# A four-block transformer kernel whose norms, projections, turned residuals and sums are signalled piece by piece

## The reference

```python
# block 0: cross attention to the 64 context tokens, 16 heads of 16
q  = ada_ln(x, cond) @ Wq + bq;  kv = ada_ln(ctx, cond) @ Wkv + bkv
x  = x + softmax(q k^T / 4) v @ Wp + bp
# block 1: evidence from the context, router over 3 experts (768 -> 512 -> 256), gate
nx = ln(x) * gamma + beta
evidence = softmax(nx Wq (ctx Wk)^T / 16) (ctx Wv)
combined = [nx, evidence, cond]
routed = sum_e router_e(combined) * expert_e(combined)
x  = x + gate(combined) * (routed @ out_w + out_b)
# block 2: full self attention over 1024 tokens, cross attention, MLP of 1024
x  = x + gate_a * (self_attention(ada(ln(x))) @ W_proj + b_proj)
x  = x + cross_attention(ln(x), ln(ctx)) @ W_cproj + b_cproj
x  = x + gate_m * (gelu(ada(ln(x)) @ W1 + b1) @ W2 + b2)
# block 3: attention in windows of 128 tokens shifted by 64,
#          cross attention to the 16 best of 64 context tokens, SwiGLU MLP of 1024
x  = x + g_msa * window_attention(ada(ln(x)))
x  = x + g_mca * topk_cross_attention(ada(ln(x)), ctx)
x  = x + g_mlp * swiglu(ada(ln(x)))
```

## Time and profile before

| what | value |
|---|---|
| device time, median of 3 runs | 1791.75 us (1786.18 to 1791.81) |
| profiled execution, its own time | 1789.12 us |
| its span, first to last instruction | 1787.0 us |
| mean granted TensorE clock | 0.951 of full speed |
| TensorE busy | 1575.8 us, 88% of the span |
| VectorE busy | 1082.2 us, 61% |
| ScalarE busy | 812.6 us, 45% |
| GpSimd busy | 417.7 us, 23% |
| transfers | 64.02 MB, mean 36 GB/s |

### The profile page before, as it was taken

How to read it: one execution, slowest core, us unless ns; L and a number is a source line. 1 busy time by engine, 2 the same in 40 slices (tenths; PEclk the granted TensorE clock), 3 DMA queues, 4 the chain that set the end, 5 groups by cost and what they waited for, 6 DMA issues and landing times.

```text
span 1787.0 us, 27133 instructions
## 1 busy us (share of the span) xinstructions
PE 1575.8 (88%) x9541; PEld 917.6 (51%) x9541; DVE 1082.2 (61%) x2933; ACT 812.6 (45%) x1283; POOL 417.7 (23%) x418
## 2 busy tenths in 40 slices
PE   3789998999988989877878899899998888987888
PEld 1536564434343756455653556543443365654566
DVE  1464243899726338799536433479991643879963
ACT  1134331388843535324533434138886353442454
POOL 0140003433006024113205000153300602412230
PEclk8799999999999999999998999999999999999899
DMA  9200004422010000000050000352201000000004
GB/s 318 95 1 1 0 1 135 61 38 38 2 71 1 1 1 2 1 1 1 1 166 2 1 1 1 111 84 38 38 2 72 1 1 1 2 1 1 1 1 141
DMA packets 43332, 64.02 MB, mean 36 GB/s; under 512 B 8634, under 2 KB 32061, under 8 KB 42301
## 3 DMA queue, kind: packets, MB, share of 16 engines
q1 hardware_dynamic: 32845, 40.73, 6.9%
q0 software_dynamic: 8448, 14.96, 5.6%
q10 hardware_dynamic: 1904, 6.55, 0.9%
HBM read 47.28 MB, written 2.10 MB: 28 GB/s over the span
## 4 chain that ended last, share of the span: by engine, by line
PE 38%; issue 37%; POOL 12%; DVE 8%; ACT 3%; SPq 2%; DMA 1%; POOLq 0%; ACTq 0%; DVEq 0%
PE ps L932 7%; PE ps L944 7%; PE ps L1188 4%; PE ps L448 3%; POOL wkblk L2396 3%; PE ps L1022 3%; PE ps L917 3%; PE ps L1030 2%; PE ps L565 2%; PE ps L1217 2%; DVE taken L2198 2%; DVE taken L2210 1%; POOL rstd L2292 1%; DVE m L2193 1%; PE ps L457 1%
## 5 line engine op out<-in xcount | busy, mean ns | idle before, releaser
L2067 DVE TENSOR_REDUCE mm<-ps 128x1 f32<-128x1024 f32 x256 | 309.6, 1223 | 36.7 <-PE ps L917 30.0
L1490 ACT ACTIVATE pt<-ps 128x512 f32<-128x512 f32 x512 | 276.9, 598 | 62.8 <-PE ps L932 53.6
L2292 POOL TENSOR_TENSOR rstd<-ve,minus_half 128x4 f32<-128x4 f32 x32 | 36.2, 1130 | 810.7 <-DVE ve L1800 810.7
L932 PE MATMUL ps<-qx,kx 64*128 64x512 f32 x512 | 192.0, 452 | 1.8 <-ACT pt L1490 1.0
L917 PE MATMUL ps<-kx,qx 48*128 48x512 f32 x512 | 189.5, 450 | 1.7 <-DVE mm L2067 1.7
L944 PE MATMUL ps<-pt,v 128*32 128x256 f32 x2048 | 161.2, 396 | 0.0
L932 PEld LDWEIGHTS ps<-qx,kx 64*128 64x128 f32 x512 | 80.0, 186 | 98.2 <-ACT pt L1490 92.9
L1956 DVE TENSOR_TENSOR rlo<-ring,rhi 128x512 fp32r<-128x512 f32 x48 | 33.2, 692 | 127.7 <-ACT ring L1441 127.6
L917 PEld LDWEIGHTS ps<-kx,qx 48*128 48x128 f32 x512 | 76.6, 187 | 25.8 <-issue 15.4
L944 PEld LDWEIGHTS ps<-pt,v 128*32 128x32 f32 x2048 | 43.3, 109 | 87.8 <-ACT pt L1490 63.7
L457 PE MATMUL ps<-ident,xhat 128*128 128x128 f32 x288 | 45.0, 309 | 44.9 <-DVE xhat L1805 43.2
(11 more groups left out here) (322 smaller groups left out, 3454.0 us busy)
## 6 DMA issues: line engine op xcount, KB each, us to landing
w<-in_L_xcond_e_w_dram SPq DMA_DIRECT2D x9, 512.0 KB, 8.0
w<-in_L_xcond_e_w_dram SPq DMA_DIRECT2D x3, 1536.0 KB, 12.1
wm<-in_L_xcond_W_mlp_dram SPq DMA_DIRECT2D x4, 1024.0 KB, 7.9
qx<-q_hi POOLq DMA_DIRECT2D x64, 64.0 KB, 2.6
kx<-k_hi POOLq DMA_DIRECT2D x64, 64.0 KB, 2.8
w3a<-in_L_xcond_w_m_dram SPq DMA_DIRECT2D x2, 2048.0 KB, 8.1
s_ada<-in_L_xcond_w_ada_dram ACTq DMA_DIRECT2D x1, 2304.0 KB, 14.7
qx<-q_lo POOLq DMA_DIRECT2D x32, 64.0 KB, 2.6
```

The source lines that it names most:

```text
L932: pe.matmul(ps[:, bank, :], kx[r, p % 4, kc * P:(kc + 1) * P], qx[r, p % 4, half * 512:(half + 1) * 512], start=True, stop=True).then_inc( ...
L1490: act.activation(pt[:, u % 8, half * 512:(half + 1) * 512], ps[:, bank, :], ACT.Exp, scale=QK_SCALE).then_inc(st_read, 1)
L2067: return dve.tensor_reduce(mm[:, p % 2, e, t:t + 1], place(), X, ALU.max).then_inc(ring_read, 1)
L2292: pool.tensor_tensor(rstd[:, k, :], ve[:, k, :], minus_half[:, :], ALU.pow).then_inc(rstd_ready, 1)
```

## The change

Semaphores that were raised once for a block, or once for two banks, are raised once for each piece, and the waits on them count pieces.

- `xhat_ready`: once for each tile. TensorE's `ln` waits for each tile and transposes both of its halves; `ln_turned` stays one for the block. `turn_block` is gone; the attention's outputs are turned half by half, with `ot_turned` raised for each.
- `hT_ready`: once for each feature half. `linear` takes a pair `each`, and waits for half c in front of its matmul on half c, in the first bank of a projection. Consumers that are not written so wait for both halves.
- Norms 4 and 7 on ScalarE: both high parts first, each with a semaphore raise (`hs2_hi`, new; `hs3_hi`), then both halves of `hT`. TensorE waits for `hs2_hi` or `hs3_hi` half by half; `tokens3_lo` waits for `hT_ready` in place of `hs3_hi`.
- `q_done` and `y_done`: once for each bank; ScalarE evicts a bank as soon as it is done. `qk3_done`: once for each of four banks.
- `yT_ready`: once for each feature half. TensorE's turn has the feature half outside and the tiles inside, and waits for each half; for residuals (0, 1), (1, 0) and (4, 0) it waits for both first (`whole`). `y_turned`: once for each PSUM bank, and VectorE adds in two instructions on 128x512, a bank each.
- Banks move: the norm behind a context attention goes to bank 2i (i: first or second), the turn of residual (5, 0) to bank 2, of (6, 0) to bank 4, of (6, 1) to bank 0, of (7, 0) to bank 2, of (7, 1) to bank 4.

The core of the diff (the waits that only count in new units are left out):

```diff
-    def linear(bank, w, m, src):
+    def linear(bank, w, m, src, each=None):
         for c in range(KC):
+            if each is not None:
+                pe.wait_ge(each[0], each[1] + c + 1)
             ins = pe.matmul(ps[:, bank, :], w[:, c, m * P:(m + 1) * P], src[:, c, :],
                             start=c == 0, stop=c == KC - 1)
         return ins
...
-            pe.wait_ge(xhat_ready, b * 2 * N_LN + 2 * i + k + 1)
-            turn_block(k, xhat, bank).then_inc(ln_turned, 1)
+            bank = 4 * k if bank is None else bank
+            for t in range(TB):
+                pe.wait_ge(xhat_ready, b * 2 * N_LN * TB + (2 * i + k) * TB + t + 1)
+                for c in range(KC):
+                    ins = pe.transpose(ps[:, bank + c, t * P:(t + 1) * P], xhat[:, TB * k + t, c * P:(c + 1) * P], ident[:, :])
+            ins.then_inc(ln_turned, 1)
         def query(i, k, ln_i, w):
-            pe.wait_ge(hT_ready, b * (2 * N_LN + 2) + ln_i + k + 1)
-            linear(4 * k + 2, w, 0, hT[:, k])
+            linear(4 * k + 2, w, 0, hT[:, k], (hT_ready, b * 2 * N_HT + 2 * (ln_i + k))).then_inc(q_done, 1)
             linear(4 * k + 3, w, 1, hT[:, k]).then_inc(q_done, 1)
-        def residual(i, k, turn, w=None, o_wait=None, src=oT, bank=None):
+        def residual(i, k, turn, w=None, o_wait=None, src=oT, bank=None, each=None, whole=False):
             if not turn:
                 bank = 4 * k + 2 if bank is None else bank
-                pe.wait_ge(*o_wait)
-                linear(bank, w, 0, src[:, k])
+                if o_wait is not None:
+                    pe.wait_ge(*o_wait)
+                linear(bank, w, 0, src[:, k], each).then_inc(y_done, 1)
                 linear(bank + 1, w, 1, src[:, k]).then_inc(y_done, 1)
             else:
                 bank = 4 * k if bank is None else bank
-                pe.wait_ge(yT_ready, b * 2 * N_RES + 2 * i + k + 1)
-                for t in range(TB):
-                    for c in range(KC):
+                for c in range(KC):
+                    if not whole or c == 0:
+                        pe.wait_ge(yT_ready, b * 4 * N_RES + 2 * (2 * i + k) + (KC if whole else c + 1))
+                    for t in range(TB):
                         ins = pe.transpose(ps[:, bank + t // 2, t % 2 * D + c * P:t % 2 * D + (c + 1) * P],
                                            yT[:, k, c, t * P:(t + 1) * P], ident[:, :])
-                ins.then_inc(y_turned, 1)
+                        if c == KC - 1 and t % 2:
+                            ins.then_inc(y_turned, 1)
...
-            residual(step, 1, False, w, (co_ready, u0 + 4), bank=4)
-            ln(step + 1, 0)
+            residual(step, 1, False, w, bank=4, each=(co_ready, u0 + KC))
+            ln(step + 1, 0, bank=2 * i)
...
-            turn_block(k, xhat).then_inc(ot_turned, 1)
+            for c in range(KC):
+                for t in range(TB):
+                    ins = pe.transpose(ps[:, 4 * k + c, t * P:(t + 1) * P], xhat[:, TB * k + t, c * P:(c + 1) * P], ident[:, :])
+                ins.then_inc(ot_turned, 1)
-        residual(2, 0, False, wproj, (hT_ready, b * (2 * N_LN + 2) + 7), hT)
-        pe.wait_ge(hT_ready, b * (2 * N_LN + 2) + 8)
-        linear(6, wproj, 0, hT[:, 1])
+        residual(2, 0, False, wproj, src=hT, each=(hT_ready, b * 2 * N_HT + 12))
+        linear(6, wproj, 0, hT[:, 1], (hT_ready, b * 2 * N_HT + 14)).then_inc(y_done, 1)
         linear(7, wproj, 1, hT[:, 1]).then_inc(y_done, 1)
...
+                    if m == 0 and (wp, sp) == (0, 0):
+                        pe.wait_ge(hs2_hi, b * NB * KC + k * KC + c + 1)
...
-                ins = linear(4 * k + m, wqkv3, m, hT[:, k])
+                linear(4 * k + m, wqkv3, m, hT[:, k], (hT_ready, b * 2 * N_HT + 2 * (12 + k)) if m == 0 else None).then_inc(qk3_done, 1)
 -                    ins.then_inc(qk3_done, 1)
...
+                            if each and (i, wp) == (0, 0):
+                                pe.wait_ge(hs3_hi, b * NB * KC + k * KC + c + 1)
...
+            def evict(dst, c):
+                if cols is None:
+                    return act.activation(dst, ps[:, bank + c, :], ACT.Copy)
+                table, scale, bias = cols
+                return affine(dst, ps[:, bank + c, :], table[:, scale + c:scale + c + 1], table[:, bias + c:bias + c + 1])
+            def high(c):
+                return hs1[:, k, c, :] if i == 1 else hs[:, k, 0, c, :] if i == 4 else hs3[k][:, c, :]
+            if i in (4, 7):
+                for c in range(KC):
+                    evict(high(c), c).then_inc(hs2_hi if i == 4 else hs3_hi, 1)
             for c in range(KC):
-                if cols is None:
-                    ins = act.activation(hT[:, k, c, :], ps[:, bank + c, :], ACT.Copy)
-                else:
-                    table, scale, bias = cols
-                    ins = affine(hT[:, k, c, :], ps[:, bank + c, :], table[:, scale + c:scale + c + 1], table[:, bias + c:bias + c + 1])
-                if i == 4:
-                    ins = affine(hs[:, k, 0, c, :], ps[:, bank + c, :], table[:, scale + c:scale + c + 1], table[:, bias + c:bias + c + 1])
-            ins.then_inc(hT_ready, 1)
+                evict(hT[:, k, c, :], c).then_inc(hT_ready, 1)
             if i == 1:
                 for c in range(KC):
-                    ins = affine(hs1[:, k, c, :], ps[:, bank + c, :], table[:, scale + c:scale + c + 1], table[:, bias + c:bias + c + 1])
+                    ins = evict(high(c), c)
                 ins.then_inc(hs1_hi, 1)
-            if i == 7:
-                for c in range(KC):
-                    ins = affine(hs3[k][:, c, :], ps[:, bank + c, :], table[:, scale + c:scale + c + 1], table[:, bias + c:bias + c + 1])
-                ins.then_inc(hs3_hi, 1)
         def query(i, k, col):
-            act.wait_ge(q_done, b * 2 * N_Q + 2 * i + k + 1)
             for c in range(KC):
+                act.wait_ge(q_done, b * 4 * N_Q + 2 * (2 * i + k) + c + 1)
                 ins = affine(qT[:, k, c, :], ps[:, 4 * k + 2 + c, :], 1.0, colT[:, col + c:col + c + 1])
             ins.then_inc(qT_ready, 1)
-        def residual(k, bank, scale, bias):
+        def residual(k, bank, scale, bias, done=None):
             for c in range(KC):
-                ins = affine(yT[:, k, c, :], ps[:, bank + c, :], 1.0 if scale is None else mod[:, scale + c:scale + c + 1],
-                             bias[:, c:c + 1])
-            ins.then_inc(yT_ready, 1)
+                if done is not None:
+                    act.wait_ge(y_done, b * 24 + 2 * done + c + 1)
+                affine(yT[:, k, c, :], ps[:, bank + c, :], 1.0 if scale is None else mod[:, scale + c:scale + c + 1],
+                       bias[:, c:c + 1]).then_inc(yT_ready, 1)
...
             for t in range(TB):
-                ins = dve.tensor_scalar(xhat[:, TB * k + t, :], x[:, TB * k + t, :], mv[:, k, t, 0:1], rstd[:, k, t:t + 1], ALU.subtract, ALU.mult)
-            ins.then_inc(xhat_ready, 1)
+                dve.tensor_scalar(xhat[:, TB * k + t, :], x[:, TB * k + t, :], mv[:, k, t, 0:1], rstd[:, k, t:t + 1], ALU.subtract, ALU.mult).then_inc(xhat_ready, 1)
         def residual(i, k, bank=None):
             bank = 4 * k if bank is None else bank
-            dve.wait_ge(y_turned, b * 2 * N_RES + 2 * i + k + 1)
-            return dve.tensor_tensor(x[:, TB * k:TB * (k + 1), :].rearrange("p t d -> p (t d)"),
-                                     x[:, TB * k:TB * (k + 1), :].rearrange("p t d -> p (t d)"),
-                                     ps[:, bank:bank + 2, :].rearrange("p a n -> p (a n)"), ALU.add)
+            for j in range(TB // 2):
+                dve.wait_ge(y_turned, b * 4 * N_RES + 2 * (2 * i + k) + j + 1)
+                two = x[:, TB * k + 2 * j:TB * k + 2 * j + 2, :].rearrange("p t d -> p (t d)")
+                ins = dve.tensor_tensor(two, two, ps[:, bank + j, :], ALU.add)
+            return ins
...
-            dve.wait_ge(y_done, b * 12 + 2 + k + 1)
             for m in range(KC):
-                ins = dve.scalar_tensor_tensor(yT[:, k, m, :], ps[:, 2 + 4 * k + m, :], colT[:, C_OUTB + m:C_OUTB + m + 1], gT[:, k, m, :], ALU.add, ALU.mult)
-            ins.then_inc(yT_ready, 1)
+                dve.wait_ge(y_done, b * 24 + 2 * (2 + k) + m + 1)
+                dve.scalar_tensor_tensor(yT[:, k, m, :], ps[:, 2 + 4 * k + m, :], colT[:, C_OUTB + m:C_OUTB + m + 1], gT[:, k, m, :], ALU.add, ALU.mult).then_inc(yT_ready, 1)
...
```

96 lines of the change are left out of this document (40 added, 56 removed).

## The result

The changed kernel takes 1738.88 us (median of 4, 1735.72 to 1745.49), the kernel before beside it 1789.12 (1786.18 to 1791.81). The ratio is 0.9722, 95% interval 0.969 to 0.9754: 50 us less. In the profiled executions 1789.12 became 1735.72.

What follows compares the result with a forecast made beforehand. TensorE, busy 88% of the span, bounds the long loops; the rest is hand-overs between stages. Terms sum to 17.3 us per batch, 34.6 in two, less 1.6 for unmet waits: 33, giving 1757 us (range 1741 to 1780).

Steps and rivals of the forecast that it cites:

- start of the batch, first residual: Earlier transposes, projection and query evictions at batch start, 2.5 us per batch; first context attention's residual add earlier, about 0.85.
- experts to attention: Between experts and attention: per-bank add gives 0.3 and the norm's turn 0.7, together 1.0 us per batch.
- norm 3 and query: Attention to second context attention: normalisation 1.35 us earlier, turn 1.0, one eviction less 0.55, query 0.5 and 0.3; 3.7 per batch.
- norm 4, both MLP blocks: Norm behind the second context attention: 0.7 us from transposes, 0.4 from high parts first, the low parts coming as before.
- window, queries and keys: Window attention, both blocks: per-bank eviction cuts TensorE's 2.5 us idle before the value projection to 0.69; 3.5 per batch.
- window to top-k: Between window and top-k: turns 0.8 us, query eviction 0.6, one norm eviction 0.6, less 0.1; 1.9 per batch.
- last MLP block 1, last add: Batch end: high parts first gain 0.6 us in the last MLP's block 1; overlapped half-turn and add gain 0.7.
- the chains named as late next: At each hand-over, the neighbouring work that would end last after the change and cap the gain, such as VectorE's own product.
- the rows that were to show them: Signs: value-projection gap about 0.7 us, norm 3's transposes within 0.1 of first tile, normalisation within 0.2 of add's end, loops unchanged.
- Norm 7's first block gains nothing: Norm 7, block 0: no gain, because fillers hold TensorE before it and GpSimd's subtraction holds it behind.
- The clock rises too: Rival: shorter gaps keep TensorE at 2.4 GHz in second value projection and query behind attention; 7.4 us more, 1749; chance 0.13.
- Slower, by the clock in the long loop: Rival: the attention loop, reached earlier, falls to 1.2 GHz; with 80 us low the time is 1797; chance 0.06.

Runs made afterwards that it cites:

- whole: The changed kernel with every piecewise wait put back to the last piece, keeping increments, split adds and moved banks: 1787.82 us, 0.9997 of the kernel before.
- the filled pair: The changed kernel, and `whole`, each with constant-tile matmuls where TensorE idles (in `whole` also in both window gaps): 1728.42 and 1768.89 us.
- gap_filled: `whole` with nine constant-tile matmuls ahead of the window stage's second value projection: 1782.22 us, 0.9967 of the kernel before.
- high: `whole` with only the high parts first in norms 4 and 7, waited for half by half: 1794.55 us, 1.0028 of the kernel before.
- whole_n7: `whole` with 13 constant-tile matmuls ahead of the turn in front of norm 7: 1797.74 us, 1.0037 of the kernel before.
- window: `whole` with only the window stage's queries and keys evicted bank by bank: 1781.45 us, 0.9981 of the kernel before.
- no_window_filled: The changed kernel with window queries and keys evicted whole again, and nine constant-tile matmuls in each window gap: 1750.16 us, 0.9777 of the kernel before.
- the first try: The changed kernel with window queries and keys evicted whole again, and 13 constant-tile matmuls ahead of norm 7: 1752.01 us, 0.9798 of the kernel before.
- warm3: The changed kernel with constant-tile matmuls at three gaps per batch, small groups at five more, and 13 ahead of norm 7: 1724.11 us, 0.9641.

## Why the prediction was too small

By the starts of GpSimd's powers, which every norm block has, and by the first and last matmul of the attention loop and the first scores of the second context attention between them, the change can be read place by place in the two profiled executions (us gained, batch 1 / batch 2):

| place | forecast | measured |
|---|---|---|
| set-up, once | 0 | 2.5 |
| start of the batch, first residual | 3.3 | 3.4 / 3.6 |
| norm 1 | 0.7 | 0.7 / 0.7 |
| experts to attention | 1.0 | 3.1 / 3.2 |
| attention loop | 0 | -0.1 / 0.8 |
| attention's outputs turned | 0 | 1.9 / -0.9 |
| norm 3 and query | 3.7 | 3.0 / 2.6 |
| second residual | 0.8 | 1.2 / 1.2 |
| norm 4, both MLP blocks | 1.1 | 2.8 / 2.4 |
| window, queries and keys | 3.5 | 4.3 / 4.3 |
| window to top-k | 1.9 | 2.8 / 4.7 |
| norm 7, block 0, and first products | 0 | 3.1 / 0.1 |
| last MLP block 1, last add | 1.3 | 0.9 / 1.2 |

The measured rows come to 27.1 and 23.9, with the set-up to 53.5 (the spans differ by 53.2; the rest is rounding); the forecast's to 17.3 twice. The medians differ by 50, since the changed kernel's profiled execution is its fastest. The set-up's 2.5 are not the change's: no edit touches it, and it took 74.9 to 77.7 over the profiled kernels, 76.0 in `whole`.

**Right: what bounds it, and the chains named as late next.** Start of batch, residuals, norm 3, window gaps and the last add came within about a us of their terms, and the rows that were to show them did: the gap in front of the values 0.78, the transposes of norm 3 0.47 behind the first tile's start (a tile takes 0.4), normalisation 0.12 behind its add's end (and 1.3 behind the end of the block's statistics, before 2.4: 1.1 gained where 1.35 was forecast), an add pair 1.28, a loop of 202.6. One term inside norm 3 was mis-sized: the turn was to end 0.4 behind the last tile and gain 1.0. It ended 1.06 behind it, before 1.40, for its eight transposes now took 1.97 and not 1.34, the low clock; 0.3 was gained.

**Right: increments are free.** `whole` has all of them and runs at 0.9997. The Trainium skill's 26.3 ns an increment (TensorE: Matmul & The Clock Gate, "The cost: per-tile semaphore tail") would have shown as 2.2 us there, 0.0012 of the time; the interval reaches 1.0006. So no such price shows in the time here.

**Failed: "Norm 7's first block gains nothing: fillers hold TensorE before it, GpSimd's subtraction behind it".** Both chains were there, but the fillers' own length wasn't looked at. They ran at the low clock in batch 1 of the kernel before, had shown such a stretch elsewhere, and batch 2 of the same trace had the fast case. A comparison of the two batches would have shown 61.1 against 58.1. Measured were 3.1 in batch 1 and 0.1 in batch 2.

**Failed: the clock as a rival instead of a term.** "The clock rises too" was priced at 7.4 at two places and given 0.13, as if it excluded the forecast. It adds to the hand-overs: the second value projection (1.7 in each batch) did come as that rival had it, the query projection behind norm 3 hardly (5.67 for 6.18). By the filled pair, 8 of the 49 against `whole` are clock at the least. The two traces allow an estimate from the places seen, both batches together: norm 7's first block 3.2, second value projections 3.4, experts stage 3.0, the projection behind norm 2's second block 2.6 (6.54 and 6.45 became 5.29 and 5.09), the MLP's first twelve matmuls 2.5 (5.17 and 4.63 became 3.66 and 3.65), the query behind norm 3 0.5. That is 15, beside the 14.7 us by which TensorE's busy time fell. So the size of the miss, 18 us, is the clock for the most part. Which of these levels the change brought about, and which another execution of the same kernel would not have, isn't shown; that of the experts stage stood in `whole` as well.

**Slightly too small at most: the hand-overs.** 33 were forecast. The filled pair gives 40.5 as an upper bound; less the 4 of the experts stage it is 36.5, and the 53.2 of the traces less the set-up's 2.5 and the 15 of clock are 36 as well (an estimate). Two rows of the table that look like it are clock beyond their forecast: experts to attention, 3.1 for 1.0, with 1.5 from the experts stage and 1.25 from the projection; and the MLP, 2.8 for 1.1, with 1.5 from its first matmuls. There, high parts first did let TensorE start 2 us earlier and VectorE's subtraction 0.65 earlier. The 4.7 for 1.9 from the window to top-k in batch 2 is not placed.

**The slower rival exists.** "Slower, by the clock in the long loop" was given 0.06. It didn't happen here, but three profiled executions (`gap_filled`, `high`, `whole_n7`) have a loop of 217 instead of 202 at a clock of 0.91. It costs 14 to 15 us at a time, there in batch 1 only; the other 31 loops profiled have 0.97 or 0.98. Of the executions that were timed, those over 12 us above their kernel's lowest are 9 of the 36 of `window`, `gap_filled` and `high`, 8 of the 12 of `whole_n7`, 1 of the 23 of the kernel before in the second set, and none of the 4 of the changed kernel. That all of them are this loop is not shown: `no_window_filled`'s profiled execution lies 12.4 above its lowest with a loop of the usual length.

**Open.** What makes that loop fall to 0.91, with the same code before it in `whole` (0.98); what decides whether the fillers ahead of norm 7 run fast, beyond how long TensorE stood before them; what sets the clock of the experts stage; and how often each level comes, since only one execution of each kernel is profiled.

## What to carry to other kernels

Signal a hand-over in pieces wherever both engines handle it in pieces anyway: the extra increments cost nothing measurable here, and each place gives its link's length less one piece, up to the chain that is late next. Price the clock of every TensorE-bound stretch as a term of the sum: compare the same stage in two iterations of a loop, since a difference between them (61.1 and 58.1 here) is what that stage may win or lose without an edit of its own. Don't judge such a part alone: the same edits brought 6 alone and 22 in company, or -6 and 11.

## What the runs showed of the hardware

- VectorE's `tensor_scalar` on 128x256 f32, four of them, took 1.38 alone and 4.55 beside GpSimd's `tensor_tensor` on 128x1024 (3.80 for two), which itself lost nothing (3.75 before). In `window` alone it was 4.53. The Trainium skill (GPSIMD Engine Reference, "Specifications") has the interfaces to SBUF shared by the two engines; the rows agree. Here VectorE pays, but not always: ahead of norm 7's first products GpSimd's `tensor_tensor` took 3.31 in batch 1 of the kernel before and 2.39 in batch 2, beside other work of VectorE.
- Fillers that are to keep the clock up are matmuls like others: behind an idle stretch of 3.2 to 3.4 us eight of them took 2.89 to 3.42 us instead of 2.08 in nine of ten batches, and held back what they were to speed up. Thirteen more ahead of them brought 2.08 in the first try; in `warm3` batch 2 and `whole_n7` batch 1 they still cost a us (59.8).
- The attention loop, in which TensorE is busy for over 98% of the time, ran at 0.97 to 0.98 of the clock (202 us) in 31 profiled cases and at 0.91 (217 us) in three, with the same code. The experts stage took 107.0 to 111.4 us at granted clocks of 0.968 to 0.923, with no match to the edits.
